# One-hots of the first stage on VectorE in three instructions per tile, and a ring of gathered rows worked off by quarters

## The reference

```python
agg = jax.ops.segment_sum(h[src], dst, num_segments=N)
z = (1.0 + eps_gin) * h + agg
z = jax.nn.relu(z @ W1 + b1) @ W2 + b2
z = (z - mean) * jax.lax.rsqrt(var + BN_EPS) * gamma + beta      # mean, var over the nodes
x = _layernorm(x + z + h)                                        # h is x
gathered = edge_val[:, None] * x[edge_col]
support = jax.ops.segment_sum(gathered, edge_row, num_segments=N)
x = _layernorm(x + jax.nn.relu(support @ weight))
```

## Time and profile before

| | us |
|---|---|
| median of 3 unprofiled runs | 4327.98 (4326.99 to 4332.28) |
| profiled execution, from first to last instruction | 5351.1 |
| PE busy in it | 3721.5 |
| POOL busy | 3177.6 |
| DVE busy | 2301.2 |
| ACT busy | 1495.5 |

### The profile page before, as it was taken

One profiled execution on the slowest core, in us unless ns is written; L12 is line 12 of the kernel. 1 busy time (PEld: TensorE's weight loads), 2 busy tenths in 40 slices (PEclk: granted clock), 3 DMA queues, 4 the chain that ended last, 5 costly groups with the idle time before them and its releaser, 6 DMA issues.

```text
span 5351.1 us, 79415 instructions
## 1 busy us (share of the span) xinstructions
PE 3721.5 (70%) x16131; PEld 3045.6 (57%) x16132; DVE 2301.2 (43%) x5448; ACT 1495.5 (28%) x4377; POOL 3177.6 (59%) x3352
## 2 busy tenths in 40 slices
PE   2677676667667776767742667777777777777777
PEld 2565555555555655656632556566665666665666
DVE  2545454545555544545563233333333333333333
ACT  2444444445444444444552000000000000000001
POOL 6666655565656665666335666666666666666662
PEclk6887888888887878888855789888888888888898
DMA  4333333333333333333293333333333333333331
GB/s 134 93 97 92 99 90 97 90 97 93 95 93 97 93 97 91 96 97 99 62 298 123 90 94 99 96 101 96 100 101 99 95 100 100 102 97 97 100 100 53
DMA packets 298112, 541.14 MB, mean 101 GB/s; under 512 B 77802, under 2 KB 190302, under 8 KB 297838
## 3 DMA queue, kind: packets, MB, share of 16 engines
q0 software_dynamic: 159424, 434.52, 28.3%
q10 hardware_dynamic: 89348, 67.77, 4.0%
q1 hardware_dynamic: 49066, 36.39, 2.2%
HBM read 489.80 MB, written 46.88 MB: 100 GB/s over the span
## 4 chain that ended last, share of the span: by engine, by line
issue 27%; ACTq 16%; another core or an unknown queue 15%; PE 15%; ACT 12%; DVE 9%; DVEq 4%; DMA 2%; SPq 1%; POOL 0%; PEldq 0%; POOLq 0%
PE ps L1419 10%; ACT ones_sb L1613 7%; DVE work L1096 7%; ACTq L1611 4%; ACTq L1613 2%; DVEq L1096 2%; PE ps L1221 2%; ACT ring L1611 2%; ACTq L1642 1%; PE ps L1459 1%; ACT ones_sb L1619 1%; ACTq L1617 1%; ACTq L377 1%; PE ps L1292 1%
## 5 line engine op out<-in xcount | busy, mean ns | idle before, releaser
L548 POOL DMA_INDIRECT ring<-in_x,idx x1664 | 1587.9, 954 | 1039.5 <-issue 456.4
L606 POOL DMA_INDIRECT ring<-x_dram,idx x1612 | 1528.0, 948 | 904.9 <-issue 479.8
L1419 PE MATMUL ps<-ring,work 128*128 x6448 | 1631.3, 411 | 581.1 <-DVE work L1096 387.5
L1419 PEld LDWEIGHTS ps<-ring,work 128*128 128x128 f32 x6448 | 1327.7, 208 | 851.0 <-issue 649.4
L1221 PE MATMUL ps<-ring,ones_sb 128*128 x3708 | 1115.7, 449 | 454.8 <-ACT ones_sb L1619 301.9
L1096 DVE TENSOR_SCALAR work<-ps,dstT,wT 128x256 f32<-128x256 f32 x1612 | 748.0, 536 | 1551.6 <-remote 977.0
L1221 PEld LDWEIGHTS ps<-ring,ones_sb 128*128 128x128 f32 x3708 | 800.4, 225 | 676.6 <-issue 550.2
L1613 ACT ACTIVATE ones_sb<-tile_nodes,dstT 128x128 f32<-128x128 f32 x1854 | 651.0, 391 | 396.5 <-issue 331.1
L1292 PE MATMUL ps<-work 128*128 128x128 f32 x3384 | 499.2, 301 | 203.6 <-issue 148.1
L1292 PEld LDWEIGHTS ps<-work 128*128 128x128 f32 x3384 | 484.0, 216 | 233.5 <-issue 189.8
L1791 ACT ACTIVATE work<-ps 128x512 f32<-128x512 f32 x49 | 29.3, 597 | 1764.2 <-remote 1111.7
(11 more groups left out here) (240 smaller groups left out, 2299.3 us busy)
## 6 DMA issues: line engine op xcount, KB each, us to landing
ring<-in_x,idx POOLq DMA_INDIRECT x1664
ring<-x_dram,idx POOLq DMA_INDIRECT x1612
z_dram<-z_pair ACTq DMA_DIRECT2D x49, 256.0 KB
ones_sb<-x_dram ACTq DMA_DIRECT2D x49, 256.0 KB
ring<-z_dram SPq DMA_DIRECT2D x24, 512.0 KB, 4.1
ring<-in_x SPq DMA_DIRECT2D x24, 512.0 KB, 5.6
x_dram<-ring ACTq DMA_DIRECT2D x24, 512.0 KB
out<-ones_sb ACTq DMA_DIRECT2D x48, 256.0 KB
```

The lines of the kernel that those rows point to most:

```text
L548: nc.gpsimd.indirect_dma_start(out=ring[:, q, c, :], out_offset=None, in_=x, in_offset=bass.IndirectOffsetOnAxis(ap=idx[:, q, c:c + 1], ax ...
L606: nc.gpsimd.indirect_dma_start(out=ring[:, q, c, :], out_offset=None, in_=x1_dram, in_offset=bass.IndirectOffsetOnAxis(ap=idx[:, q, c:c + ...
L1419: last = nc.tensor.matmul(to[:, t * D:(t + 1) * D], ones_of[:, b, c, t * P:(t + 1) * P], ring[:, ds((p + b) & (RING - 1), 1), c, :].rearra ...
```

## The change

VectorE takes over the one-hots of stage one. Destinations are stored negated (`dstT`); one `scalar_tensor_tensor` adds the tile's first node to them and compares with minus the column number. There are three per tile: the shared pair (2 x 128 columns), the eight heads at once (16 x 128), the last pair (2 x 128), more only if a tile has loop pairs. They stand in `block` between the halves of `keyed` and after `take`. The self weights are copied by POOL, eight pairs in one instruction after each 16 gathers, from `self_next`, which SyncE loads beside the indices. SyncE reports eight pairs at a time in both stages; POOL waits for the room of four pairs. TensorE waits once for all of a tile's heads' one-hots, and for rows at half of the heads and at the tile's end. ScalarE keeps the copies out of PSUM and is one step nearer to TensorE. In stage two VectorE makes a bucket's first four loop pairs as soon as the previous bucket's loop is added. The table is in 16-bit integers.

```diff
@@ tables
-        NEW, HEAD, M4, M2, END, OFF, COL, REP, PREV, MID = range(10)
-        NEW2, M42, HEAD2, M22, END2 = range(5)
-        MOST = PADP * NT
+        NEW, HEAD, M4, M2, END, LOW, REP, SHARED, OFF, SWEEP = range(10)
+        NEW2, M42, HEAD2, M22, END2, PREV2 = range(6)
+        MOST = max(ROUNDS * NT, PADP, TILE_ONES * NT)
-        table = sb("table", [1, NT, 10], i32)
+        table = sb("table", [1, NT, 10], mybir.dt.uint16)
@@ SyncE, stage one
-                        for g in range(RING // TWO):
-                            sp.wait_ge(s_gathered[g], r * (32 * TWO) + 32 * TWO)
-                            sp.sem_inc(s_landed, TWO)
-                            if (g + 1) * TWO % HALF == 0:
+                        for g in range(4):
+                            sp.wait_ge(s_gathered[g], r * (32 * QUARTER) + 32 * QUARTER)
+                            stand(sp)
+                            sp.wait_ge(s_selfed, r * 4 + g + 1)
+                            sp.sem_inc(s_landed, QUARTER)
+                            if g % 2 == 1:
...
+                                sp.dma_start(self_next[:, h * HALF:(h + 1) * HALF, :],
+                                             selfT[:, ds((i + 1) * RING + h * HALF, HALF), :]).then_inc(s_idx[h], 16)
@@ SyncE, stage two
-                for g in range(RING // TWO):
-                    with sp.If(r * RING + g * TWO < pairs2):
-                        sp.wait_ge(s_row2[g], r * (32 * TWO) + 32 * TWO)
-                        sp.sem_inc(s_landed2, TWO)
+                for g in range(4):
+                    with sp.If(r * RING + g * QUARTER < pairs2):
+                        sp.wait_ge(s_row2[g], r * (32 * QUARTER) + 32 * QUARTER)
+                        sp.sem_inc(s_landed2, QUARTER)
@@ POOL, stage one
+            def selves_of(q, of):
+                nc.gpsimd.tensor_copy(ring_self[:, q:q + QUARTER, :], of[:, q:q + QUARTER, :]).then_inc(s_selfed, 1)
+
+            pool.wait_ge(s_selves, 1)
+            for q in range(0, RING, QUARTER):
+                selves_of(q, selfT)
...
-                        if q % TWO == 0:
-                            pool.wait_ge(s_entered, r * RING + (q - RING + 3))
+                        if q % FOUR == 0:
+                            pool.wait_ge(s_entered, r * RING + (q - RING + FOUR + 1))
                             stand(pool)
                         for c in range(2):
                             gather(q, c)
+                        if (q + 1) % QUARTER == 0:
+                            selves_of(q + 1 - QUARTER, self_next)
@@ POOL, stage two
-                    for q in range(h * HALF, (h + 1) * HALF, TWO):
+                    for q in range(h * HALF, (h + 1) * HALF, QUARTER):
...
-                            pool.wait_ge(s_added2, r * RING + q + 2)
-                            stand(pool)
-                            for b in range(TWO):
-                                for c in range(2):
-                                    gather2(q + b, c)
+                            for f in range(q, q + QUARTER, FOUR):
+                                pool.wait_ge(s_added2, r * RING + f + FOUR)
+                                stand(pool)
+                                for b in range(FOUR):
+                                    for c in range(2):
+                                        gather2(f + b, c)
@@ VectorE, stage one
+            def ones_of_tile(j, bank):
+                new, head, m4, m2, _, _, _, shared, off, sweep = entry(dve, j)
+                counted = sweep * RING + off
+                base = tile_base[:, j:j + 1] if isinstance(j, int) else tile_base[:, ds(j, 1)]
+
+                def equal(to, at, n):
...
+                    return nc.vector.scalar_tensor_tensor(
+                        out=to.rearrange("p b c n -> p (b c) n"),
+                        in0=dstT[:, ds(at, n), :].rearrange("p b c -> p (b c)").unsqueeze(2).to_broadcast([P, 2 * n, P]),
+                        scalar=base, in1=minus_iota[:, :].unsqueeze(1).to_broadcast([P, 2 * n, P]), op0=ALU.add, op1=ALU.is_equal)
+
+                if not (isinstance(j, int) and j < 2):
+                    dve.wait_ge(s_acc, j - 1)
+                    stand(dve)
+                equal(shared_of[bank], shared, 1).then_inc(s_onehot, 1)
+                with dve.If(new < m4):
...
+                            dve.wait_ge(s_added, p + counted + (TILE_ONES + b - TWO))
+                            stand(dve)
+                            equal(loop_of[:, b:b + TWO], p + b, TWO).then_inc(s_onehot, TWO)
...
+                equal(heads_of[bank], head, BATCH)
+                equal(last_of[bank], m2, 1).then_inc(s_onehot, TILE_ONES - 1)
...
                 members(k)
                 if old >= 1:
-                    keyed(k - 1)
+                    keyed(k - 1, range(PARTS // 2))
+                ones_of_tile(2 * k + 1, 1)
+                if old >= 1:
+                    keyed(k - 1, range(PARTS // 2, PARTS))
                 if old >= 5:
                     z_stats(k - 5)
                 places(k, fore)
                 take(k)
-
+                ones_of_tile(2 * k + 2, 0)
@@ VectorE, stage two
                 with dve.If(new < m4):
-                    with dve.Fori(new, m4, 2 * TWO) as p:
+                    dve.wait_ge(s_added2, prev_head + RING)
+                    stand(dve)
+                    for b in range(0, 2 * TWO, TWO):
+                        weighted(loop2[:, b:b + TWO], new + b, TWO)
+                with dve.If(new + 2 * TWO < m4):
+                    with dve.Fori(new + 2 * TWO, m4, 2 * TWO) as p:
@@ TensorE, sum_tile
+                pe.wait_ge(s_onehot, head + counted + TILE_ONES)
+                pe.wait_ge(s_landed, low + first)
+                stand(pe)
                 for g in range(HEADS):
+                    if g == HEADS // 2:
+                        pe.wait_ge(s_landed, end + first)
+                        stand(pe)
@@ ScalarE: ones_of_tile (with far, near), before_first, before_second, within_second deleted
+            def two_tiles(k, old, sorts=True, loads=True):
+                if old >= 3:
+                    z_out(k - 3)
+                if sorts:
+                    ranks_out(k)
+                summed(k, 0)
+                if loads:
+                    load_x(k + 1)
+                if old >= 2:
+                    hidden_out(k - 2)
...
```

More of the change, by code:

```diff
@@ L287, in gnn @@
         s_table = sem("s_table")
-        s_gathered = [sem(f"s_gathered{g}") for g in range(RING // TWO)]
+        s_gathered = [sem(f"s_gathered{g}") for g in range(4)]
+        s_selfed = sem("s_selfed")
         s_landed = sem("s_landed")
@@ L351, in gnn @@
         s_idx2 = [sem(f"s_idx2_{h}") for h in range(2)]
-        s_row2 = [sem(f"s_row2_{g}") for g in range(RING // TWO)]
+        s_row2 = [sem(f"s_row2_{g}") for g in range(4)]
         s_landed2 = sem("s_landed2")
@@ L693, in _ @@
             setup(nc.vector.tensor_tensor(rep, newly, tmp, ALU.subtract))
-            setup(nc.vector.memset(begins, 1.0))
             setup(nc.vector.tensor_tensor(two_i, new, newly, ALU.subtract))
+            setup(nc.vector.tensor_tensor(spare, new, newly, ALU.subtract))
             sync()
-            setup(nc.vector.tensor_tensor_scan(off, begins, rep, 0.0, ALU.mult, ALU.add))
             setup(nc.vector.tensor_scalar(news_i, two_i, 1, None, ALU.arith_shift_right))
+            setup(nc.vector.tensor_scalar(tmp, sweep_f[0:1, 0:NT], flag[0:1, 0:1], None, ALU.mult))
             sync()
@@ L859, in take, with keyed @@
                 stand(dve)
-            def keyed(k):
-                for q in range(PARTS):
+            def keyed(k, parts):
+                for q in parts:
                     mine = slice(q * WIDTH, (q + 1) * WIDTH)
@@ L1089, in steps2 @@
             def steps2(j):
-                new, m4, head, m2, end = entry2(dve, j)
+                new, m4, head, m2, end, prev_head = entry2(dve, j)
                 def weighted(to, p, n):
@@ L1206, in sum_tile @@
             def sum_tile(j, bank, others):
-                new, head, m4, m2, end, off, _, rep, _, _ = entry(pe, j)
+                new, head, m4, m2, end, low, rep, _, off, sweep = entry(pe, j)
+                first = sweep * RING
+                counted = first + off
                 if not (isinstance(j, int) and j < 2):
@@ L1222, in add @@
                                                     start=False, stop=False)
-                            if is_new and b == n - 1 and c == 0:
+                            if b == n - 1 and c == 0:
                                 last.then_inc(s_entered, n)
-                    last.then_inc(s_added, n)
+                    return last
                 with pe.If(rep > 0):
-                    add(new - 1, shared_of[bank], 1, False)
+                    pe.wait_ge(s_onehot, new + counted + 1)
+                    for c in range(2):
```

(7 more changed lines are left out.)

209 lines of the change are left out of this document (74 added, 135 removed).

## The result

The changed kernel takes 4500.22 us (median of 4 runs, 4496.78 to 4502.72); the kernel before took 4327.48 in the same comparison (4325.63 to 4332.28). The ratio is 1.0396, 95% interval 1.0381 to 1.041: 173 us slower, inside the range of 4370 to 4690 and 48 us under the forecast of 4548.

What follows compares the result with a forecast made beforehand. The prediction took POOL's gather pace to bound the kernel nearly throughout. Its terms, 150 + 7 + 42 + 5 + 10 + 6 + 10 = 230 less 10, gave +220 us: 4548 us, range 4370 to 4690.

Steps and rivals of the forecast that it cites:

- POOL's pace is the bound: Both stages, unprofiled: 3276 gathers at 1.254 us need 4108 us; with 234 us of rest, 4342 against the median 4328.
- The 1023 us: Difference between profiled execution (5351.1 us) and median, taken as standing of POOL that the recorded run adds.
- The heads hold gathers: Stage one: gathers begun u after a heads instruction's start wait for its end; 1.53 us each, 150 over 98 tiles.
- The short ones: Stage one's two short one-hot instructions per tile catch a gather one time in four: 7 us, perhaps 32 more.
- POOL's copies: 104 self-weight copies on POOL at 0.4 us each: 42 us, bounds 21 and 130.
- Ends: Quarters: four extra gathers 5 us, stage two's last quarter 10, stage one's last quarter 6, POOL's stand at start 10.
- ScalarE's relief: One-hots leaving ScalarE in stage one: waits lie inside POOL's pace, so 10 us saved, at most 30.
- (a): Rival: VectorE or the lag takes over in stage one, 50 us a step; about 4720 us, chance 0.15.
- (b): Rival: VectorE's instructions stall gathers only briefly, leaving only copies and ends; 4391 us, chance 0.09 shared with (e).
- (e): Rival: the change doesn't do what it says, say the gather's index read slips out early; as (b), sharing chance 0.09.
- (c): Rival: faster; unrecorded POOL pace under about 1.2 us, consumers bound, ScalarE's relief about 100 us; 4230 us, chance 0.15.
- (d): Rival: relief of (c) and half of the stalls cancel, within 9 us of 4328; chance 0.05.

Runs made afterwards that it cites:

- before_fewer: Kernel before with 16-bit tables, with the second gather of every eighth stage-two pair left out (100 gathers): 4206.77 us, ratio 0.9715.
- before_16: Kernel before with its two tables in 16-bit integers, nothing else: 4331.46 us, ratio 1.0004; recorded span 4334.6 us.
- after: The changed kernel itself, against the kernel before: 4500.22 us, ratio 1.0396; recorded span 4494.7 us.
- before_hold: Kernel before with 16-bit tables, plus 94 unused VectorE instructions of 1536 elements with both tensors in SBUF: 4446.11 us, ratio 1.0269.
- after_copies2: Changed kernel with a second same-size POOL copy after each of the 100 in the loop: 5357.2 us, ratio 0.9953, on a slow chip.
- after_best: Changed kernel with minus iota in PSUM, stage two's ring by groups of two pairs, and earlier first POOL copies: 4371.03 us, ratio 1.0076.
- after_psum_b: Changed kernel with minus iota, second tensor of VectorE's first-stage one-hots, in PSUM instead of SBUF: 4400.07 us, ratio 1.0146.

## Why the prediction was right, step by step

**POOL's pace is the bound: right.** before_fewer measured 1.25 us per gather left out, and before_16's trace shows 1252 ns as the median pitch in the loop of stage one. The estimate of 4342 us without standing lay within 8 us of that trace's span, 4334.6, and 11 of its median; its 195 us between the stages (237 less 42) measured 183.5, its gathers 4114 for 4108.

**The 1023 us as something that the recorded run adds: wrong.** before_16 was recorded without them, and unprofiled runs on two chips have them. The argument from the rows (a full ring in the trace, 4108 + 234 in the median) was good and found that profile and median show two bounds; the cause given was not. It had a consequence: the span of after was foretold near 5250, and it was 4494.7.

**The heads hold gathers: right, size 123 us for 150.** In the trace of after all 98 heads instructions caught a gather. Each ended 0.81 to 0.85 us after the instruction (median 0.819, predicted 0.82). The instructions took 2.352 us in the median (predicted 2.30). A hold was 1.25 us where 1.53 was reckoned, because u was not spread evenly over 0 to 1.25: its mean was 0.99 us and not 0.625, and a late u is a short hold. Part of this can be read. In 27 of the 98 cases a gather had begun 0.05 to 0.09 us after the start of the heads instruction, and it took its usual 0.95 us. The next, begun 1.30 to 1.34 us after that start, was held, and the VectorE instruction itself took 2.37 to 2.41 us. From 0.097 us on, every gather was held. So the prediction's sentence that a gather begun inside waits for the end fails at the very start of the instruction, and there u is 1.3. The short instruction directly ahead may shift u as well (a gather begun within it is prolonged, as the one at 1194.42), but no run tested that. In before_hold, where no such instruction stands ahead, u's mean was 0.48 and the hold nearly what that gives.

**The short ones: 7 predicted, 7 measured.** Of 196, some 50 caught a gather, and 39 of these gathers were prolonged, by 7.1 us together. The last one-hot did not prolong the hold of the heads. In the loop as a whole the sum doesn't show, since before_16 has some 11 us of its own that after has not: gathers begun within VectorE's sorting, most of them within line 778, an addition with both inputs in SBUF.

**POOL's copies: 42 us predicted, 6 to 10 measured. The mis-sized term.** The group view of POOL in the trace of after:

```profile
L566 POOL COPY ring<-self_next 128x16 f32<-128x16 f32 x100 | 22.1, 221 | 0.3
```

A copy takes 0.22 us, but it goes into most of the gap of 0.30 that stands ahead of every gather: in the timeline above, the copy ends at 1191.74 and the next gather begins at 1191.89. Across a copy the step is 1.316 us in place of 1.251. That is 0.065 us times some 100. The gather behind a copy is a little longer besides, 0.977 us for 0.946, another 3 us. The value taken, 0.4, gave the copy a gap of its own; the lower bound was 0.20, so the measured 0.07 to 0.10 lies below the bounds given. (The prediction's signs name 108 copies near 0.15 us; there are 104, of 0.22.) No run tested the term where POOL sets the pace: after_copies2 fell on a crawling chip, and the figure is read from the trace of after.

**Ends: 31 predicted (5 + 10 + 6 + 10), 32 measured (2 + 13 + 8 + 9).** The start shows in the waits as predicted: gather 65 at 102.1 in place of 93.0. The 13 us at the end are stage two's last quarter; after_best, without it, has 30.9 of 43.3. Of the 8 between the stages the prediction named the quarter only, at 6; the sizes meet by luck. TensorE's last product ends 14 us later after the last gather than in before_16, and its one wait of 21.8 us for ScalarE, behind VectorE's queue, is longer than that. How much of the 8 is stage one's quarter was not measured. This queue was missing from the prediction. It listed what the one-hots cost VectorE and what they do to POOL, but not what stands behind them on VectorE at the end of the stage.

**ScalarE's relief: 10 taken, nothing seen.** ScalarE is busy for 413.3 us in place of 1495.5 (before_16: 1456.3), and no term of the time follows it on the chips of the comparison. The same goes for fewer waits on SyncE and POOL.

**Rivals.** (a) did not come in the loop: VectorE is busy 304 to 318 us of each 400 there, and after_psum_b goes at POOL's pace with all of VectorE's new work. It was near, though. With the holds gone TensorE waits 285 us for VectorE's one-hots (44 in after), and at the end of the stage VectorE's lateness is paid. (b) and (e) fell with the held gathers. (c) fell with before_fewer: the pace without recording is 1.25. (d), no change, fell with the median.

The sum of the measured terms: 123 (holds) + 7 (short ones) + 10 (copies) + 32 (ends), less some 11 that only before_16 has in its loop, = 161, against 160 between the spans and 173 between the medians. The forecast of 220 was 59 above this sum: 32 too much for the copies, 27 for the size of the holds and 11 for what before_16 loses itself, less the 10 of relief that did not come and 1 at the ends. The 13 us by which the medians differ more than the spans are those named under the table: 6 + 3 + 4. That the forecast came within 48 us of the median owes something to them; against the spans it was 60 too high.

## What to carry to other kernels

When one engine's steady stream of short instructions sets the pace, ask of every instruction put on a neighbour what it locks; here the moved work was free in the loop for its time on VectorE, and cost 1.2 us for each long instruction with two SBUF inputs; placing one operand in PSUM removed that. Look at what stands behind moved work on an in-order queue at the end of a stage, where no loop hides it. And compare the profiled execution's span with the unprofiled times before reading waits from it: if they differ by a quarter, its bound may not be that of the median, and a second recorded run, on another chip where there is one, settles it cheaply.

## What was not expected of the hardware

- The same program takes 4330 us on some chips and 5377 to 5421 on others, unprofiled, with granted clocks of 0.94 to 0.95 and about 0.83 in the records. On the slow ones TensorE has gaps that nothing in the profile explains.
- A POOL copy of 16 elements between two indirect gathers adds 0.065 us to a step, for 0.22 us of work, and the gather behind it takes 0.03 us more.
- All 98, and in the other kernel all 94, long VectorE instructions with two SBUF inputs held a gather until 0.82 us after their end. A gather begun within the first 0.09 us of such an instruction was not held (27 of 27), and the instruction was then 0.02 to 0.06 us longer.
- The clock granted over the whole of after was 0.875 and of before_16 0.943, with POOL's pitch the same (1.251 and 1.252): on POOL's pace the lower clock had no effect.
